# Attention-and-FFN kernel: a new order of some steps around the first two feed-forward groups, one low part moved from GpSimd to VectorE, and the last output stored in halves

## The chip, the cores and the metric

The kernel runs on one core of one Trainium2 chip. The metric is the device time of one launch in microseconds (us). The kernel before took 103.91 us, the median of three runs.

## The reference

The input x has 16 sequences of 128 tokens with 256 channels. The layer adds a weighted running mean over time (an RWKV "wkv" recurrence whose keys are the normalised x and whose values are `ctx_2048`), and then a gated feed-forward block with 704 hidden channels:

```python
# per sequence; k = layernorm(x), v = ctx_2048, C = 256 channels
def step(carry, kv_t):                      # over the 128 tokens
    aa, bb, pp = carry
    ww = u + kt
    q = maximum(pp, ww)
    y_t = (exp(pp - q) * aa + exp(ww - q) * vt) / (exp(pp - q) * bb + exp(ww - q))
    ...
x = x + wkv(time_decay, time_first, layernorm(x), ctx_2048)
n = layernorm(x)
g = (n @ gate_w.T) * gate_s                 # 704 hidden channels, weights -1, 0 or 1
u = (n @ up_w.T) * up_s
x = x + ((silu(g) * u) @ down_w.T) * down_s
```

## The kernel before

**Tiling.** Two sequences make a unit (256 tokens; 8 units), two units make a group (512 tokens; 4 groups). The 704 hidden channels are 5 full tiles of 128 and one rest of 64. A hidden tile has a running number n, from 0 to 23 over the whole program: group n // 6, tile n % 6 within it; 5, 11, 17 and 23 are the rests.

**Attention part of unit u.** ScalarE: `expk(u)` makes the exponentials `ek`. TensorE transposes them (`e_T(u)`, into `ps_a`) and, for units 0 to 3, also their products with v (`p_T(u)`, into `ps_b`; units 4 to 7 use VectorE's `mulp(u)` for that). VectorE runs two scans over time (`scan_e`, `scan_p`) and forms `denom(u)` and `numer(u)`. ScalarE makes the reciprocal (`log_den`, `recip`), GpSimd multiplies (`divide(u)`) and adds to the residual (`add_y(u)`).

**Second layernorm of unit u.** TensorE transposes the sum back (`x1_T(u)`), VectorE takes its statistics (`stats2`, `aggr2`), GpSimd and ScalarE form scale and bias, ScalarE normalises (`norm2(u)`), TensorE transposes again (`n_T(u)`). The result is kept as two float32r numbers: ScalarE copies it into the high part `xh` (`high_n(u)`), VectorE subtracts that from the original and writes the low part `xl` (`low_n(u)`).

**Feed-forward part.** For tile n TensorE multiplies high and low parts by the gate and the up weights (`gate(n)`, `up(n)`, four matmuls each, into a ring of three PSUM banks `ps_f`), ScalarE takes the silu, VectorE multiplies (`gated(n)`, into `h`), ScalarE makes the high part of the result (`high_h(n)`, into `hh`), GpSimd the low part (`low_h(n)`, into `hl`); for the rest tiles VectorE makes the low part (`low_rest(n)`, into `hx`). `down(n)` adds both parts' products to `ps_d`, which has two halves of 128 output channels, c = 0 and c = 1. From n = 20 on `down(n)` does c = 0 alone and `downb(n)` does c = 1. At the end of a group VectorE adds the result to `xc` (`residual`), and SyncE's queue stores it, one DMA per half. Of the first three products (gate 0, up 0, gate 1) the first 256 tokens are done ahead of the others, as `gatea(0)`, `upa(0)`, `gatea(1)`; these need only unit 0.

**What sets the order.** Each engine runs a list written out by hand, in its own queue, and waits on semaphores. An instruction that waits holds up all that stands behind it on its engine. The waits that matter here:

- `p_T(u)` waits until `numer(u - 1)` is done, since it overwrites `ps_b`; `e_T(u)` waits for `denom(u - 1)` in the same way.
- `gatea(0)` waits for `low_n(0)`; the other half of `gate(0)` waits for `low_n(1)`; `gate(6)`, the first of the next group, waits for `low_n(3)`.
- `gated(n)` waits for `up(n)` and the silu. A product waits until the ring's bank that it takes has been read: `gate(2)` for `gated(0)`, `gate(3)` for `gated(1)`, `gate(7)` for `low_rest(5)`.
- `down(22)` waits for the low part of tile 22; `down(23)` and `downb(23)` for `low_rest(23)`.

Of the kernel before, what the change touches and what calls it, by code (L numbers as in the profile page):

```python
# [51 lines left out]
HS = 4  # L52
# [5 lines left out]
def build(nc, x_tok, x_ch, v_tok, v_ch, w_gu, w_d, vecs, out_ch):  # L58
    with ExitStack() as ctx:  # L59
# [6 lines left out]
        def sem(name):  # L66
            return ctx.enter_context(nc.semaphore(name))
# [147 lines left out]
        def wait_low(eng, n):  # L215

            g, m = divmod(n, MC)
            if m < FULL:
                eng.wait_ge(s_hl, FULL * g + m + 1)
            else:  # L220
                eng.wait_ge(s_hx, g + 1)
# [3 lines left out]
        @block.sync  # L225
        def _(sp):
            def load_x(u):
                sp.dma_start(xt[:, seqs(u), :], x_tok[seqs(u), :, :].rearrange("b t c -> t b c")).then_inc(s_xt[u], 16)  # L228

            def load_v(k):  # L230

                g = k - GU + 1
                if k < GU or g < TOK_UNITS // GU:
                    bs = seqs(k) if k < GU else slice(g * GU * UB, (g + 1) * GU * UB)
                    sp.dma_start(vt[:, bs, :], v_tok[bs, :, :].rearrange("b t c -> t b c")).then_inc(s_vt[k], 16)
                else:
# [24 lines left out]
        def _(pool):
# [104 lines left out]
            rstd2(3); bias1(7); low_h(4); divide(4); add_y(4); rstd2(4); divide(5); add_y(5); low_h(6); low_h(7)  # L366
            rstd2(5); low_h(8); first(3); divide(6); add_y(6); low_h(9); low_h(10); rstd2(6); divide(7); add_y(7)
            low_h(12); low_h(13); rstd2(7); low_h(14); low_h(15); low_h(16); low_h(18); low_h(19); low_h(20)
            low_h(21); low_h(22)

        @block.scalar
        def _(act):
# [115 lines left out]

            rstd1(0); expk(0); elift_(); rstd1(1); expk(1); rstd1(3); log_den(0); expk(2); recip(0); wcheck(0)
            log_den(1); recip(1); wcheck(1); wcheck(2); log_den(2); recip(2); expk(3); rstd2a(0); rstd1(5); rstd2a(1)  # L490
            norm2(0); norm2(1); expk(4); high_n(0); log_den(3); high_n(1); expk(5); recip(3); tables(SILU); silu(0)
            silu(1); high_h(0); norm2(2); silu(2); high_h(1); silu(3); high_h(2); high_n(2); silu(4); high_h(3)
            silu(5); tables(LN_EXP); log_den(4); rstd1(7); high_h(4); recip(4); norm2(3); expk(6); high_n(3); expk(7)
            log_den(5); high_h(5); recip(5); tables(SILU); silu(6); silu(7); norm2(4); high_h(6); silu(8); high_n(4)
            high_h(7); silu(9); tables(LN_EXP); log_den(6); recip(6); high_h(8); norm2(5); tables(SILU); silu(10)
            high_n(5); high_h(9); silu(11); high_h(10); silu(12); high_h(11); tables(LN_EXP); log_den(7); recip(7)
            tables(SILU); silu(13); norm2(6); silu(14); high_n(6); high_h(12); silu(15); high_h(13); high_h(14)
# [5 lines left out]
        def _(dve):  # L503
# [115 lines left out]
            def gated(n):  # L619
# [6 lines left out]
                if m < FULL and n >= HS and (n - HS) % MC < FULL:  # L626
# [4 lines left out]
                nc.vector.scalar_tensor_tensor(h[:, n % HS, :] if m < FULL else up, up, vec[r, V_US + m:V_US + m + 1],  # L631
                                               sil[r, n % 2, :], ALU.mult, ALU.mult).then_inc(s_h, 1)

            def low_rest(n):
                wait_high(dve, n)
                if n >= MC:
                    dve.wait_ge(s_dn, CC * (n - MC + 1))
                nc.vector.tensor_tensor(hx[0:REST, :], ps_f[REST:P, slot(n, 1) % RING, :], hx[REST:P, :].bitcast(F32),
                                        ALU.subtract).then_inc(s_hx, 1)

            def residual(g, c):
                ts = slice(g * GT, (g + 1) * GT)
                nc.vector.scalar_tensor_tensor(xc[:, c, ts], ps_d[:, c, :], vec[:, V_DS + c:V_DS + c + 1],
                                               xc[:, c, ts], ALU.mult, ALU.add).then_inc(s_fin, 1)

            def finish(g):
# [5 lines left out]
            def finish_c(c):  # L652

                dve.wait_ge(s_x1, UNITS)
                dve.wait_ge(s_tail[c], 1)
                residual(GROUPS - 1, c)

            lift_(); stats1(0); aggr1(0); stats1(1); stats1(2); decay_(); aggr1(1); aggr1(2); stats1(3); scan_e(0)
            aggr1(3); denom(0); scan_p(0); scan_e(1); numer(0); denom(1); scan_p(1); scan_e(2); numer(1); denom(2)
            stats1(4); stats1(5); stats2(0); aggr1(4); aggr1(5); aggr2(0); stats2(1); publish(); aggr2(1); scan_e(3)  # L660
            scan_p(2); denom(3); numer(2); stats1(6); low_n(0); scan_p(3); low_n(1); numer(3); stats2(2); mulp(4)
            aggr2(2); gated(0); gated(1); scan_p(4); scan_e(4); gated(2); stats1(7); gated(3); low_n(2); numer(4)
            denom(4); aggr1(6); stats2(3); aggr1(7); aggr2(3); gated(4); gated(5); mulp(5); scan_e(5); scan_p(5)
            denom(5); low_n(3); numer(5); stats2(4); low_rest(5); aggr2(4); scan_e(6); gated(6); mulp(6); gated(7)
            finish(0); low_n(4); denom(6); stats2(5); aggr2(5); gated(8); gated(9); scan_p(6); numer(6); scan_e(7)
            low_n(5); gated(10); gated(11); mulp(7); stats2(6); denom(7); low_rest(11); gated(12); aggr2(6); scan_p(7)
            numer(7); gated(13); finish(1); low_n(6); gated(14); stats2(7); aggr2(7); gated(15); gated(16); gated(17)
            low_n(7); low_rest(17); gated(18); gated(19); finish(2); gated(20); gated(21); gated(22); gated(23)
            low_rest(23); finish_c(0); finish_c(1)

        @block.tensor
        def _(pe):
# [92 lines left out]
            def rest_of_program(exact):  # L765
                def gate(n):
                    product(n, 0, exact, 1 if slot(n, 0) < HALVED else None)

                def up(n):
                    product(n, 1, exact, 1 if slot(n, 1) < HALVED else None)  # L770

                def gatea(n):
                    product(n, 0, exact, 0)

                def upa(n):
                    product(n, 1, exact, 0)
# [72 lines left out]
```

## Time and profile before

| what | value |
|---|---|
| median of three runs | 103.91 us (103.79 to 104.14) |
| the profiled execution | 104.59 us, of which its span is 102.7 us |
| PE (TensorE) busy | 91.5 us, 89% of the span |
| DVE (VectorE) busy | 80.0 us, 78% |
| ACT (ScalarE) busy | 78.2 us, 76% |
| POOL (GpSimd) busy | 66.8 us, 65% |

All times within the span count from its start. PE's matmuls are pipelined: the printed duration of one is longer than the distance to the next, so its pace is read from start to start. On ACT and DVE an instruction may start some 0.1 us before the end printed for the one ahead of it.

### The profile page before, as it was taken

How to read it: one execution, taken by the hardware profiler on the slowest of the kernel's cores; microseconds unless marked ns; L12 is line 12 of the kernel's file. 1: busy time of each engine (PE TensorE's matmuls, PEld its weight loads, DVE VectorE, ACT ScalarE, POOL GpSimd, SP SyncE). 2: the span in 40 equal slices, each digit the busy share in tenths (PEclk: the TensorE clock that was granted, in tenths of full speed). 3: DMA queues.
4: the chain of work that ended last, by engine and by line, in shares of the span. 5: the costliest groups of instructions: out<-in, count | busy, mean ns of one | idle time of the engine just before them, and what ended most of it. 6: DMA issues, size and time to landing. Idle time of an engine off the chain costs nothing.

```text
span 102.7 us, 1698 instructions
## 1 busy us (share of the span) xinstructions
PE 91.5 (89%) x504; PEld 75.1 (73%) x504; DVE 80.0 (78%) x169; ACT 78.2 (76%) x136; POOL 66.8 (65%) x96
## 2 busy tenths in 40 slices
PE   3958976998799999996999999999999999999930
PEld 3957965996596778875788887887888778888610
DVE  1789899969998999799999998999863806543450
ACT  4371999989997879999999999999959634655300
POOL 2016465998799999894399779827899701764500
PEclk9999999999999999999999999999999999999999
DMA  1999999999000000000005000000500000400005
GB/s 32 307 379 405 403 321 388 343 387 343 34 0 0 0 0 10 0 0 0 0 0 203 1 6 0 0 3 0 203 1 0 0 6 3 183 21 0 0 28 189
DMA packets 6475, 10.78 MB, mean 105 GB/s; under 512 B 576, under 2 KB 3648, under 8 KB 6336
## 3 DMA queue, kind: packets, MB, share of 16 engines
q1 hardware_dynamic: 6320, 10.62, 28.9%
q8 instruction: 6, 0.10, 0.4%
q10 hardware_dynamic: 144, 0.03, 0.2%
q14 instruction: 5, 0.04, 0.1%
HBM read 8.55 MB, written 2.10 MB: 104 GB/s over the span
## 4 chain that ended last, share of the span: by engine, by line
PE 27%; POOL 17%; ACT 15%; issue 14%; DMA 11%; DVE 6%; SPq 4%; POOLq 2%; DVEq 1%; ACTq 0%
PE ps_f L728 16%; DMA xc<-x_ch 11%; POOL hl L346 11%; PE ps_d L745 4%; ACT ek L405 4%; PE ps_f L756 3%; ACT L374 2%; POOL xc L311 2%; ACT nt L434 2%; SPq L228 2%; PE ps_x L698 2%; ACT xh L445 2%; DVE h L631 1%; POOL rs L323 1%; POOLq L59 1%
## 5 line engine op out<-in xcount | busy, mean ns | idle before, releaser
L728 PE MATMUL ps_f<-xh,wgu_r 128*128 128x512 f32 (+1 forms) x94 | 36.3, 391 | 0.6 <-DVE xl L616 0.4
L728 PE MATMUL ps_f<-xl,wgu_r 128*128 128x512 f32 (+1 forms) x94 | 35.1, 378 | 0.0
L346 POOL TENSOR_TENSOR hl<-h,hh 128x512 fp32r<-128x512 f32 x20 | 25.6, 1293 | 9.3 <-ACT hh L476 9.2
L631 DVE SCALAR_TENSOR_TENSOR h<-ps_f,vec,sil 128x512 f32<-128x512 f32 x20 | 14.9, 744 | 9.2 <-PE ps_f L728 6.2
L728 PEld LDWEIGHTS ps_f<-xh,wgu_r 128*128 128x128 f32 x94 | 17.7, 188 | 5.5 <-issue 1.4
L728 PEld LDWEIGHTS ps_f<-xl,wgu_r 128*128 128x128 f32 x94 | 17.7, 188 | 2.8
L756 PE MATMUL ps_f<-ident 128*128 128x128 f32 x110 | 15.5, 296 | 1.9 <-POOL ident L266 1.6
L465 ACT ACTIVATE sil<-ps_f,vec 128x512 f32<-128x512 f32 x20 | 13.7, 688 | 4.0 <-PE ps_f L728 3.8
L745 PE MATMUL ps_d<-hh,wd_r 128*128 128x512 f32 x40 | 16.3, 407 | 0.1
L756 PEld LDWEIGHTS ps_f<-ident 128*128 128x128 f32 x110 | 14.5, 211 | 2.1 <-POOL ident L266 1.6
L476 ACT ACTIVATE hh<-h 128x512 fp32r<-128x512 f32 x20 | 12.5, 629 | 4.6 <-DVE h L631 4.5
L745 PE MATMUL ps_d<-hl,wd_r 128*128 128x512 f32 x40 | 15.7, 393 | 0.0
L305 POOL TENSOR_TENSOR yk<-num,rden 128x508 f32<-128x508 f32 x8 | 10.2, 1281 | 2.1 <-DVE num L593 1.5
L374 ACT ACT_TABLE_LOAD x8 | 10.3, 1283 | 1.3 <-PEq L843 1.2
L405 ACT ACTIVATE ek<-xt,nb,rs 128x256 f32<-128x256 f32 x16 | 8.7, 595 | 2.9 <-POOL nb L283 2.8
L311 POOL TENSOR_TENSOR xc<-xc,yk 128x508 f32<-128x508 f32 x8 | 10.3, 1282 | 0.6
L558 DVE TENSOR_TENSOR_SCAN sbe<-decay,ps_a 128x512 f32<-128x512 f32 x8 | 9.6, 1204 | 0.4 <-PE ps_a L679 0.4
L569 DVE TENSOR_TENSOR_SCAN sbp<-decay,ps_b 128x512 f32<-128x512 f32 x8 | 9.6, 1205 | 0.0
L745 PEld LDWEIGHTS ps_d<-hh,wd_r 128*128 128x128 f32 x40 | 7.5, 188 | 2.2 <-POOL hl L346 0.7
L745 PEld LDWEIGHTS ps_d<-hl,wd_r 128*128 128x128 f32 x40 | 7.5, 189 | 1.4
L434 ACT ACTIVATE nt<-ps_x,nb,rs 128x256 f32<-128x256 f32 x14 | 7.1, 557 | 0.8 <-POOL nb L327 0.7
L679 PE MATMUL ps_a<-ident,ek 128*128 128x128 f32 x32 | 5.1, 281 | 2.4 <-ACT ek L405 2.2
(73 smaller groups left out, 133.8 us busy)
## 6 DMA issues: line engine op xcount, KB each, us to landing
xt<-x_tok SPq DMA_DIRECT2D x8, 256.0 KB, 7.3
xc<-x_ch SPq DMA_DIRECT2D x4, 512.0 KB, 9.6
out_ch<-xc SPq DMA_DIRECT2D x8, 256.0 KB, 2.5
wgu<-w_gu SPq DMA_DIRECT2D x1, 1408.0 KB, 8.6
vc<-v_ch SPq DMA_DIRECT2D x2, 512.0 KB, 9.4
wd<-w_d SPq DMA_DIRECT2D x1, 768.0 KB, 10.0
vt<-v_tok SPq DMA_DIRECT2D x2, 256.0 KB, 5.3
vt<-v_tok SPq DMA_DIRECT2D x1, 512.0 KB, 12.3
```

What stands on the lines that cost most here:

```text
L305: nc.gpsimd.tensor_tensor(yk[:, u % 2, :, 1:T], num[:, u % 2, :, 1:T], rden[:, u % 2, :, 1:T], ALU.mult).then_inc(s_y, 1)
L311: nc.gpsimd.tensor_tensor(later(xc, u), later(xc, u), yk[:, u % 2, :, 1:T].rearrange("p (c b) t -> p c b t", c=CC), ALU.add).then_inc(s_x1, 1)
L346: nc.gpsimd.tensor_tensor(hl[:, m, :], h[:, n % HS, :], hh[:, m, :].bitcast(F32), ALU.subtract).then_inc(s_hl, 1)
L374: nc.scalar.preload_act_table_set(name)
L405: last = nc.scalar.activation(ek[:, b, :], xt[:, b, :], ACT.Exp, scale=rs1[:, b:b + 1], bias=nb1[:, b:b + 1])
L465: nc.scalar.activation(sil[:, n % 2, :], f, ACT.Silu, scale=vec[:, V_GS + m:V_GS + m + 1]).then_inc(s_sil, 1)
L476: nc.scalar.activation(hh[:, m, :], h[:, n % HS, :], ACT.Copy).then_inc(s_hh, 1)
L558: nc.vector.tensor_tensor_scan(sbe[:, u % 2, :, :].rearrange("p q t -> p (q t)"), decay[:, :, :].rearrange("p q t -> p (q t)"), ps_a[:, :, ...
L631: nc.vector.scalar_tensor_tensor(h[:, n % HS, :] if m < FULL else up, up, vec[r, V_US + m:V_US + m + 1], sil[r, n % 2, :], ALU.mult, ALU.m ...
L728: last = nc.tensor.matmul(ps_f[:, i % RING, ts], w, a, start=c == 0 and x is xh, stop=c == CC - 1 and x is xl)
L745: last = nc.tensor.matmul(ps_d[:, c, :], wd_r[:, m, cs] if exact else wd[:, m, cs], a if exact else a.bitcast(F32), start=m == 0 and i == ...
L756: nc.tensor.matmul(ps_f[:, RING - 1, 0:P], ident[:, :], ident[:, :], start=True, stop=True)
```

## The change

Five things are edited.

1. **First group, ScalarE and VectorE.** `high_n(0)` now stands ahead of `expk(4)`, and `high_n(1)` ahead of `log_den(3)`. On VectorE `low_n(0)` stands ahead of `numer(2)`, and `low_n(1)` ahead of `scan_p(3)`; `stats1(6)` moves behind `scan_p(3)`.
2. **First group, TensorE.** `e_T(4)` moves from ahead of `p_T(3)` to behind `upa(0)`, and `x1_T(2)` from ahead of `gate(0)` to behind `gate(1)`.
3. **Second group.** `low_n(3)` stands ahead of `denom(5)`, `high_h(5)` ahead of `log_den(5)`, and `gate(6)` ahead of `e_T(6)` and `x1_T(4)`.
4. **Last low part.** The low part of tile 22 is made by VectorE, in a new function `low_last`, with its own semaphore `s_hld`.
5. **End.** The products for c = 0 of tile 23 are done ahead of those for c = 1 of tile 22. The last residual for c = 1 is added and stored in two halves of 256 tokens.

```diff
+LOW_DVE = 22
...
+            if n == LOW_DVE:
+                eng.wait_ge(s_hld, 1)
+            elif m < FULL:
                 eng.wait_ge(s_hl, FULL * g + m + 1)
...
+            for i, (c, a, b) in enumerate(((0, 0, GT), (1, 0, UT), (1, UT, GT))):
+                sp.wait_ge(s_fin, done + i + 1)
+                store(c, slice(last + a, last + b))
...
-            low_h(21); low_h(22)
+            low_h(21)
...
-            norm2(0); norm2(1); expk(4); high_n(0); log_den(3); high_n(1); expk(5); recip(3); tables(SILU); silu(0)
+            norm2(0); norm2(1); high_n(0); expk(4); high_n(1); log_den(3); expk(5); recip(3); tables(SILU); silu(0)
...
-            log_den(5); high_h(5); recip(5); tables(SILU); silu(6); silu(7); norm2(4); high_h(6); silu(8); high_n(4)
+            high_h(5); log_den(5); recip(5); tables(SILU); silu(6); silu(7); norm2(4); high_h(6); silu(8); high_n(4)
...
+            def low_last(n):
+
+                g, m = divmod(n, MC)
+                wait_high(dve, n)
+                dve.wait_ge(s_dn, CC * (n - MC + 1))
+                nc.vector.tensor_tensor(hl[:, m, :], h[:, n % HS, :], hh[:, m, :].bitcast(F32),
+                                        ALU.subtract).then_inc(s_hld, 1)
...
+                if c == 0:
+                    residual(GROUPS - 1, c)
+                else:
+                    residual(GROUPS - 1, c, slice(0, UT))
+
+            def finish_d(c):
+
+                residual(GROUPS - 1, c, slice(UT, GT))
...
-                warm(2); n_T(0); warm(1); n_T(1); e_T(4); p_T(3); gatea(0); upa(0); gatea(1); x1_T(2); gate(0); gate(1); up(0); up(1)
+                warm(2); n_T(0); warm(1); n_T(1); p_T(3); gatea(0); upa(0); e_T(4); gatea(1); gate(0); gate(1); x1_T(2); up(0); up(1)
...
-                downb(22); down(23); downb(23)
+                down(23); downb(22); downb(23)
```

VectorE around the low parts of the first group, before (`den` is `denom(3)`, the two `num` are `numer(2)` and `numer(3)`, `st<-xt` is `stats1(6)`, the two `xl` are `low_n(0)` and `low_n(1)`, `sbp` is `scan_p(3)`, `st<-ps_x` is `stats2(2)`):

```order
L583 SCALAR_TENSOR_TENSOR den<-ps_a,fcol,sbe 128x2x127 x2
L593 SCALAR_TENSOR_TENSOR num<-ps_b,fcol,sbp 128x2x127 x2
L533 BN_STATS st<-xt 128x6 x2
L616 TENSOR_TENSOR xl<-ps_x,xh 128x2x256
L569 SCALAR_TENSOR_TENSOR sbp<-decay,ps_b 128x512
L616 TENSOR_TENSOR xl<-ps_d,xh 128x2x256
L593 SCALAR_TENSOR_TENSOR num<-ps_b,fcol,sbp 128x2x127 x2
L600 BN_STATS st<-ps_x 128x6 x2
```

The same place in the changed kernel (its line numbers are higher):

```order
L594 SCALAR_TENSOR_TENSOR den<-ps_a,fcol,sbe 128x2x127 x2
L627 TENSOR_TENSOR xl<-ps_x,xh 128x2x256
L604 SCALAR_TENSOR_TENSOR num<-ps_b,fcol,sbp 128x2x127 x2
L627 TENSOR_TENSOR xl<-ps_d,xh 128x2x256
L580 SCALAR_TENSOR_TENSOR sbp<-decay,ps_b 128x512
L544 BN_STATS st<-xt 128x6 x2
L604 SCALAR_TENSOR_TENSOR num<-ps_b,fcol,sbp 128x2x127 x2
L611 BN_STATS st<-ps_x 128x6 x2
```

`low_n(0)` has moved ahead of `numer(2)`, `low_n(1)` ahead of the scan, and `stats1(6)` behind it; the number of instructions is the same.

TensorE at the start of the second group, before (`ps_d<-` is `down(4)`, then `e_T(6)`, `x1_T(4)`, and the first two matmuls of `gate(6)`):

```order
L745 MATMUL ps_d<-hh,wd_r 128x512
L745 MATMUL ps_d<-hl,wd_r 128x512
L679 MATMUL ps_a<-ident,ek 128x128 x4
L698 MATMUL ps_x<-ident,xc 128x128 x4
L728 MATMUL ps_f<-xh,wgu_r 128x512
L728 MATMUL ps_f<-xl,wgu_r 128x512
```

The same place in the changed kernel:

```order
L771 MATMUL ps_d<-hh,wd_r 128x512
L771 MATMUL ps_d<-hl,wd_r 128x512
L754 MATMUL ps_f<-xh,wgu_r 128x512
L754 MATMUL ps_f<-xl,wgu_r 128x512
L754 MATMUL ps_f<-xh,wgu_r 128x512
L754 MATMUL ps_f<-xl,wgu_r 128x512
L705 MATMUL ps_a<-ident,ek 128x128 x4
L724 MATMUL ps_x<-ident,xc 128x128 x4
```

The four matmuls of `gate(6)` now stand ahead of both sets of transposes.

## Rows read from the trace of the kernel before

**Rows 1.** Windows: length, busy time (and instructions) of each engine, clock, DMA share, GB/s.

```profile
48.26:96.60 48.34, 48.34 (x229) 39.06 (x227) 35.49 (x63) 38.28 (x59) 31.91 (x38) 1.00 0.09 34
```

**Rows 2.** Timeline of ACT, first group: start, duration, engine, line, instruction.

```profile
25.31 1.09 ACT L405 ACTIVATE ek<-xt,nb,rs 128x256 f32<-128x256 f32 x2
26.30 0.59 ACT L445 ACTIVATE xh<-ps_x 128x512 fp32r<-128x512 f32 x1
...
30.88 1.27 ACT L465 ACTIVATE sil<-ps_f,vec 128x512 f32<-128x512 f32 x2
```

**Rows 3.** Timeline of DVE, first group.

```profile
25.80 0.86 DVE L593 SCALAR_TENSOR_TENSOR num<-ps_b,fcol,sbp 128x254 f32<-128x254 f32 x2
...
27.24 0.67 DVE L616 TENSOR_TENSOR xl<-ps_x,xh 128x512 fp32r<-128x512 f32 x1
27.83 1.21 DVE L569 TENSOR_TENSOR_SCAN sbp<-decay,ps_b 128x512 f32<-128x512 f32 x1
...
30.32 0.75 DVE L600 BATCH_NORM_STATS2 st<-ps_x 128x6 f32<-128x256 f32 x2
...
31.86 0.72 DVE L631 SCALAR_TENSOR_TENSOR h<-ps_f,vec,sil 128x512 f32<-128x512 f32 x1
```

**Rows 4.** Timeline of PE, first group; brackets give idle time before.

```profile
26.95 0.60 PE L688 MATMUL ps_b<-ident,vt 128*128 128x128 f32 x4
27.97 0.39 PE L728 MATMUL ps_f<-xh,wgu_r 128*128 128x256 f32 x1 [0.42 <-DVE xl L616]
...
29.49 0.61 PE L698 MATMUL ps_x<-ident,xc 128*128 128x128 f32 x4
29.86 0.36 PE L728 MATMUL ps_f<-xh,wgu_r 128*128 128x256 f32 x1
...
32.73 0.47 PE L728 MATMUL ps_f<-xh,wgu_r 128*128 128x512 f32 x1
...
33.90 0.47 PE L728 MATMUL ps_f<-xh,wgu_r 128*128 128x512 f32 x1
```

**Rows 5.** Timeline of PE, second group.

```profile
47.28 0.63 PE L679 MATMUL ps_a<-ident,ek 128*128 128x128 f32 x4 [0.85 <-ACT ek L405]
...
48.26 0.48 PE L728 MATMUL ps_f<-xh,wgu_r 128*128 128x512 f32 x1
...
50.18 0.40 PE L728 MATMUL ps_f<-xh,wgu_r 128*128 128x512 f32 x1
```

**Rows 6.** Timeline of ACT, second group.

```profile
45.67 0.58 ACT L445 ACTIVATE xh<-ps_x 128x512 fp32r<-128x512 f32 x1
```

**Rows 7.** Timeline of DVE, second group.

```profile
46.28 0.85 DVE L583 SCALAR_TENSOR_TENSOR den<-ps_a,fcol,sbe 128x254 f32<-128x254 f32 x2
47.05 0.68 DVE L616 TENSOR_TENSOR xl<-ps_x,xh 128x512 fp32r<-128x512 f32 x1
...
49.33 0.69 DVE L638 TENSOR_TENSOR hx<-ps_f,hx 64x512 fp32r<-64x512 f32 x1
```

**Rows 8.** Timeline of POOL, PEld and PE at the end.

```profile
95.48 1.30 POOL L346 TENSOR_TENSOR hl<-h,hh 128x512 fp32r<-128x512 f32 x1 [1.89 <-ACT hh L476]
...
96.39 0.39 PE L745 MATMUL ps_d<-hl,wd_r 128*128 128x512 f32 x1
96.83 0.19 PEld L745 LDWEIGHTS ps_d<-hh,wd_r 128*128 128x128 f32 x1 [0.49 <-POOL hl L346]
...
97.86 0.63 PE L745 MATMUL ps_d<-hx,wd_r 128*128 128x512 f32 x2
```

**Rows 9.** Timeline of DVE at the end.

```profile
96.21 0.69 DVE L638 TENSOR_TENSOR hx<-ps_f,hx 64x512 fp32r<-64x512 f32 x1 [0.66 <-ACT hx L478]
98.36 1.41 DVE L643 SCALAR_TENSOR_TENSOR xc<-ps_d,vec,xc 128x512 f32<-128x512 f32 x2 [1.46 <-PE ps_d L745]
```

**Rows 10.** The page, DMA issues: instruction, count, size of each, median us to landing.

```profile
out_ch<-xc SPq DMA_DIRECT2D x8, 256.0 KB, 2.5
```

**Rows 11.** Windows just before the end: columns as in the first group.

```profile
100.00:100.50 0.50, 0.00 (x0) 0.00 (x0) 0.00 (x0) 0.00 (x0) 0.00 (x0) 1.00 1.00 373
```

More of the change, by code:

```diff
@@ L156, in build @@
             "s_gate", "s_up", "s_sil", "s_h", "s_hh", "s_hhp", "s_hl", "s_hx", "s_dn", "s_fin", "s_set", "s_res"))
+        s_hld = sem("s_hld")
         s_tail = [sem(f"s_tail{c}") for c in range(CC)]
@@ L217, in wait_low @@
             g, m = divmod(n, MC)
-            if m < FULL:
+            if n == LOW_DVE:
+                eng.wait_ge(s_hld, 1)
+            elif m < FULL:
                 eng.wait_ge(s_hl, FULL * g + m + 1)
@@ L248, in _, with store @@
             load_x(6); load_x(7); load_v(4); load_res(2); load_res(3)
-            for g in range(GROUPS):
+            def store(c, ts):
+                sp.dma_start(out_ch[c * P:(c + 1) * P, ts], xc[:, c, ts]).then_inc(s_out, 16)
+            for g in range(GROUPS - 1):
                 for c in range(CC):
@@ L255, in _ @@
                         sp.wait_ge(s_fin, CC * (g - len([i for i in FIN_ACT if i < g])) + c + 1)
-                    sp.dma_start(out_ch[c * P:(c + 1) * P, g * GT:(g + 1) * GT],
-                                 xc[:, c, g * GT:(g + 1) * GT]).then_inc(s_out, 16)
-            sp.wait_ge(s_out, 16 * GROUPS * CC)
+                    store(c, slice(g * GT, (g + 1) * GT))
+            done = CC * (GROUPS - 1 - len(FIN_ACT))
+            last = (GROUPS - 1) * GT
+            for i, (c, a, b) in enumerate(((0, 0, GT), (1, 0, UT), (1, UT, GT))):
+                sp.wait_ge(s_fin, done + i + 1)
+                store(c, slice(last + a, last + b))
+            sp.wait_ge(s_out, 16 * (GROUPS * CC + 1))
         @block.gpsimd
@@ L639, in low_rest, with residual @@
                                         ALU.subtract).then_inc(s_hx, 1)
-            def residual(g, c):
-                ts = slice(g * GT, (g + 1) * GT)
-                nc.vector.scalar_tensor_tensor(xc[:, c, ts], ps_d[:, c, :], vec[:, V_DS + c:V_DS + c + 1],
+            def residual(g, c, cols=slice(0, GT)):
+                ts = slice(g * GT + cols.start, g * GT + cols.stop)
+                nc.vector.scalar_tensor_tensor(xc[:, c, ts], ps_d[:, c, cols], vec[:, V_DS + c:V_DS + c + 1],
                                                xc[:, c, ts], ALU.mult, ALU.add).then_inc(s_fin, 1)
@@ L655, in finish_c @@
                 dve.wait_ge(s_tail[c], 1)
-                residual(GROUPS - 1, c)
+                if c == 0:
[4 more added lines that the diff above has]
+                residual(GROUPS - 1, c, slice(UT, GT))
             lift_(); stats1(0); aggr1(0); stats1(1); stats1(2); decay_(); aggr1(1); aggr1(2); stats1(3); scan_e(0)
@@ L660, in _ @@
             stats1(4); stats1(5); stats2(0); aggr1(4); aggr1(5); aggr2(0); stats2(1); publish(); aggr2(1); scan_e(3)
-            scan_p(2); denom(3); numer(2); stats1(6); low_n(0); scan_p(3); low_n(1); numer(3); stats2(2); mulp(4)
+            scan_p(2); denom(3); low_n(0); numer(2); low_n(1); scan_p(3); stats1(6); numer(3); stats2(2); mulp(4)
             aggr2(2); gated(0); gated(1); scan_p(4); scan_e(4); gated(2); stats1(7); gated(3); low_n(2); numer(4)
             denom(4); aggr1(6); stats2(3); aggr1(7); aggr2(3); gated(4); gated(5); mulp(5); scan_e(5); scan_p(5)
-            denom(5); low_n(3); numer(5); stats2(4); low_rest(5); aggr2(4); scan_e(6); gated(6); mulp(6); gated(7)
+            low_n(3); denom(5); numer(5); stats2(4); low_rest(5); aggr2(4); scan_e(6); gated(6); mulp(6); gated(7)
             finish(0); low_n(4); denom(6); stats2(5); aggr2(5); gated(8); gated(9); scan_p(6); numer(6); scan_e(7)
@@ L668, in _ @@
             low_n(7); low_rest(17); gated(18); gated(19); finish(2); gated(20); gated(21); gated(22); gated(23)
-            low_rest(23); finish_c(0); finish_c(1)
+            low_last(22); low_rest(23); finish_c(0); finish_c(1); finish_d(1)
         @block.tensor
@@ L782, in downb @@
                     down_(n, exact, (1,))
-                warm(2); n_T(0); warm(1); n_T(1); e_T(4); p_T(3); gatea(0); upa(0); gatea(1); x1_T(2); gate(0); gate(1); up(0); up(1)
+                warm(2); n_T(0); warm(1); n_T(1); p_T(3); gatea(0); upa(0); e_T(4); gatea(1); gate(0); gate(1); x1_T(2); up(0); up(1)
                 gate(2); gate(3); up(2); up(3); n_T(2); gate(4); gate(5); x1_T(3); down(0); up(4); e_T(5); down(1)
-                down(2); down(3); n_T(3); down(4); e_T(6); x1_T(4); gate(6); up(6); gate(7); down(5); up(7); gate(8)
+                down(2); down(3); n_T(3); down(4); gate(6); e_T(6); x1_T(4); up(6); gate(7); down(5); up(7); gate(8)
                 n_T(4); gate(9); up(8); x1_T(5); down(6); up(9); e_T(7); gate(10); gate(11); down(7); n_T(5); up(10)
```

## The prediction

> **What bounds the kernel now.** I read the windows first. From 48.26 us to 96.60 us TensorE is busy for 48.34 us of 48.34 at full clock, while VectorE is busy for 35.49 and ScalarE for 38.28 [rows 1]. So from 48.26 on the end is set by two things: when TensorE enters this run, and what follows it. Time lost ahead of 48.26 is not won back inside the run, since there is no idle time in it. Then I read the timelines of the three places that the edits touch. Ahead of the run the engines wait for each other in turn, and a step that is late on one is late on all; the chain of waits runs there through ScalarE, TensorE and VectorE.
>
> **First group: what the new order does.** On ScalarE `expk(4)` starts at 25.31 and `high_n(0)` at 26.30 [rows 2]. Swapped, `high_n(0)` starts at 25.31 and ends 0.59 later, at 25.90. That is 0.99 us earlier. What ScalarE has to do before the first silu is the same work in another order, so that silu stays near 30.88 [rows 2].
>
> On VectorE `numer(2)` starts at 25.80 in the kernel before [rows 3]. Now `low_n(0)` is ahead of it and waits for the high part, to 25.97 (a hand-over of 0.07, my estimate from rows that sit between 0.04 and 0.11). It holds the engine for 27.83 - 27.24 = 0.59 [rows 3], so `numer(2)` runs from 26.56 to 27.42, which is 0.76 later than before.
>
> On TensorE the queue still has `p_T(3)` ahead of `gatea(0)`, and `p_T(3)` waits for `numer(2)`. It starts at 27.48 instead of 26.95 [rows 4]. Four transposes hold TensorE for some 0.49, so `gatea(0)` starts at 27.97. It started at 27.97 before [rows 4]. The early low part buys nothing here: another wait takes the place of the one removed.
>
> Behind it the queue has now three half products and `e_T(4)`, then two half products, then `x1_T(2)`. Three half products took 29.49 - 27.97 = 1.52 with a slow first one, and then about 0.47 each; a set of transposes takes 29.86 - 29.49 = 0.37 [rows 4], and the first product behind one about 0.55. The sum: 27.97 + 0.55 + 0.47 + 0.37 + 0.55 + 0.47 + 0.47 = 30.85, the start of `x1_T(2)`. It was 29.49 [rows 4]. Its input is no tighter: `add_y(2)` is late by the 0.76 of `numer(2)`, which would allow 30.25. The last transpose ends 0.61 after the first began, at 31.46 [rows 4].
>
> VectorE takes the statistics behind it. They started at 30.32, and `gated(0)` at 31.86 [rows 3], so 1.54 lie between, with `mulp(4)` among it. Now: 31.46 + 0.04 + 1.54 = 33.04 for `gated(0)`, 1.18 later. `gate(2)` needs the bank that `gated(0)` reads; it started 0.15 behind the end of that, 32.73 [rows 3, 4], and now starts at 33.04 + 0.72 + 0.15 = 33.91. `gate(3)` had to wait until 33.90 for `gated(1)` [rows 4]; now `gated(1)` is done by about 34.5 and `gate(3)` follows `gate(2)` at once, at 33.91 + 1.0 = 34.91. As it starts without a pause it saves 0.1 of the start-up. So TensorE is **0.91 us late** from here. From here to 48.26 the steps hang on each other (silu on the gate product, gated on both, the next product on gated), so I let it pass on in full. Bounds: 0.58, if `x1_T(2)` cost nothing and only `numer(3)`, done at about 30.85, held the statistics back; 1.18 if the pause before `gate(3)` stays.
>
> **Second group.** ScalarE's high part of unit 3 ends at 45.67 + 0.58 = 46.25 [rows 6], and VectorE reaches this place at 46.28 [rows 7]. In the new order `low_n(3)` goes first, from 46.32 to 47.00, and `gate(6)` starts at 47.06 instead of 48.26 [rows 5]. That fills 0.85 of idle time [rows 5]. But `e_T(6)` and `x1_T(4)` stand behind it: `gate(6)` holds TensorE for 1.0, the first transposes 0.35, so `x1_T(4)` starts at 48.41 and ends 0.61 later, at 49.02. VectorE's `stats2(4)` starts at 49.05 and takes 0.75 [rows 3], then `low_rest(5)` runs from 49.84 to 50.53; it ran from 49.33 to 50.02 [rows 7]. `gate(7)` must wait for it. `up(6)` is done by 49.8, but `gate(7)` starts only at 50.6 instead of 50.18 [rows 5]; with the start-up after a pause TensorE is **0.50 us late**, on top of the other. The early `high_h(5)` does not help, since the statistics stand ahead of `low_rest(5)` and not it. Bounds: 0 (the place is hidden if `low_rest(5)` needs nothing of `x1_T(4)`; it does by the queue) and 0.6.
>
> **End.** GpSimd's low part of tile 22 runs from 95.48 to 96.78; TensorE is free at 96.39 + 0.23 = 96.62 and waits to 96.83 for it [rows 8]. VectorE sits idle for 0.66 before 96.21 [rows 9], that is from 95.55. A low part there takes 0.67 to 0.69 [rows 3, 7] with one input in PSUM; this one has both in SBUF, and no row shows that on VectorE. I take 0.69: from 95.5 to 96.2, holding the engine for 0.60, so `low_rest(23)` keeps its 96.21 and `down(22)` starts at 96.62. Bounds: 0.67, and GpSimd's 1.30 [rows 8], which would make `low_rest(23)` 0.6 late. The Trainium skill speaks against this edit: GPSIMD Engine Reference, Key points, says that GpSimd and VectorE contend for SBUF when a VectorE instruction has two SBUF inputs. By that rule the 1.30 would be nearer if GpSimd were at work; its list ends with tile 21 now, so nothing of its own is running.
>
> Then c = 0: two matmuls of tile 22 and one of 23, 96.62 + 3 x 0.23 = 97.31 free, result at 97.48; its residual starts at 97.58, half of 1.41 long [rows 9], to 98.28. For c = 1 three more matmuls end at 98.17. The first half of its residual starts at 98.28. Two pieces of 254 took 0.86 [rows 3], so both halves are done at 98.28 + 0.86 = 99.14. Before, the last residual ended at 98.36 + 1.41 = 99.77 [rows 9]. That is 0.63 won, of which 0.21 comes from the low part, and the rest from c = 0 no longer being in the way of c = 1.
>
> The last store has half the size. A store of 256 KB lands 2.5 us after issue [rows 10]; at 373 GB/s [rows 11] 128 KB are 0.35 us of it. I take 0.35; at least nothing is won. The skill's DMA: Bandwidth & Descriptors (Anatomy of one DMA) gives a fixed part of some 2.0 us and bytes over 436e9: by it the half is worth 0.30, a sum 0.05 higher than mine. Together **0.98 us won**.
>
> **The sum.** 0.91 + 0.50 - 0.98 = +0.43 us. The profiled execution took 104.59 for a span of 102.7; it would take 105.0. That execution is 0.7% above the median of 103.91, so the median goes to 103.91 + 0.43 = 104.34. One part in 300, 0.31 us, is about what a measurement of this kernel can tell from no change; +0.43 is just beyond it.
>
> **The rivals.**
> - *The wait in the first group is hidden* (faster). Place: between 33 and 46 us. If ScalarE's chain to the second group (exponentials, high part, 25 to 46 us) and not TensorE's products were what really sets 48.26, the 0.91 is absorbed where ScalarE still has work in hand. For it: ScalarE is on the chain of waits for most of this stretch. Against it: ScalarE's own silus there wait for the products. It decides at a slack of 0.91 between the first gated tiles and ScalarE's next exponentials. Sum 0.50 - 0.98 = -0.48: 103.4; with both slips absorbed -0.98: 102.9.
> - *The second group costs nothing*, since statistics of unit 4 come early enough or `gate(7)` is not held. Sum 0.91 - 0.98 = -0.07: 103.8. For it: 0.85 of TensorE's idle time is filled. It decides at `low_rest(5)` ending by the time that `up(6)` is done.
> - *The end gives less*: the half store lands no sooner, +0.78: 104.7. With a slow low part on VectorE (1.30) the 0.21 is lost and c = 0 waits 0.5 for `low_rest(23)`: about 105.1.
> - *The moves do nothing*: the waits only change places and no start moves. That is the first rival with both slips absorbed, 102.9, and its chance is in there.
>
> **Chances.** Both slips and the gain at the end: 0.50, with its own range 104.0 to 104.8. Absorbed, one or both: 0.21. No cost in the second group: 0.17. The end gives less: 0.12. Within the likeliest case some 0.12 falls under 104.22, the border of slower. So slower 0.38 + 0.12 = 0.50; within 0.3% 0.12 + 0.15 = 0.27, as most of the third case is there; faster 0.21 + 0.02 = 0.23. The range goes down into the first rival and up to the last: 103.1 to 104.9.
>
> **What the profile will show.** Right: `gatea(0)` starts where it did, near 28.0; `x1_T(2)` near 30.9; `gated(0)` near 33.0; TensorE idle about 1 us before `gate(2)`; `gate(6)` well ahead of `e_T(6)`, then idle time of some 0.8 before `gate(7)` with `low_rest(5)` as its releaser; no idle time before `down(22)`; the last residual half 0.6 sooner behind the last matmuls. Wrong: TensorE's unbroken run starts no more than 0.5 later than 48.26 and 50.18 did, or `gated(0)` starts before 32.3. What would upset it most is that TensorE, held up early, had slack that I do not see, or that a set of transposes ends sooner than modelled.

## The result

The changed kernel is slower: 105.09 us (median of five runs) against 104.03 us, a ratio of 1.0104 with a 95% interval of 1.0079 to 1.0128, or 0.82 to 1.33 us. The ratio compares means, and leaves out one execution of each kernel (105.54 and 106.77 us) that took some 1.5 us longer than the others. Forecast were 104.34 us, 0.43 us more than before, and a range of 103.1 to 104.9. So the direction was right, but the size was too small by more than half, and the time lies above the range. The profiled execution took 105.4 us with a span of 103.6 us.

The first group in the changed kernel, timeline of VectorE (start, duration, engine, line, instruction; brackets: idle time before and its releaser). These rows answer to [rows 3].

```profile
26.04 0.68 DVE L627 TENSOR_TENSOR xl<-ps_x,xh 128x512 fp32r<-128x512 f32 x1
26.64 0.86 DVE L604 SCALAR_TENSOR_TENSOR num<-ps_b,fcol,sbp 128x254 f32<-128x254 f32 x2
...
31.55 0.76 DVE L611 BATCH_NORM_STATS2 st<-ps_x 128x6 f32<-128x256 f32 x2 [0.54 <-PE ps_x L724]
...
33.11 1.38 DVE L642 SCALAR_TENSOR_TENSOR h<-ps_f,vec,sil 128x512 f32<-128x512 f32 x2
```

The same in TensorE's timeline; they answer to [rows 4].

```profile
27.64 0.63 PE L714 MATMUL ps_b<-ident,vt 128*128 128x128 f32 x4 [1.48 <-DVE num L604]
28.03 0.37 PE L754 MATMUL ps_f<-xh,wgu_r 128*128 128x256 f32 x1
...
30.92 0.60 PE L724 MATMUL ps_x<-ident,xc 128*128 128x128 f32 x4
...
33.97 0.47 PE L754 MATMUL ps_f<-xh,wgu_r 128*128 128x512 f32 x1 [1.06 <-DVE h L642]
...
34.97 0.39 PE L754 MATMUL ps_f<-xh,wgu_r 128*128 128x512 f32 x1
```

The reader sees the steps of the forecast one by one. `low_n(0)` ends early, but `p_T(3)` waits 1.48 us for `numer(2)`, so `gatea(0)` starts at 28.03 and not earlier than in [rows 4]. `x1_T(2)` starts at 30.92 (forecast 30.85), VectorE waits 0.54 for it, `gated(0)` starts at 33.11 (forecast 33.04), and TensorE is idle for 1.06 us before `gate(2)`.

The second group, TensorE and VectorE, for [rows 5] and [rows 7]:

```profile
48.00 0.50 PE L754 MATMUL ps_f<-xh,wgu_r 128*128 128x512 f32 x1 [0.60 <-DVE xl L627]
...
51.66 0.50 PE L754 MATMUL ps_f<-xh,wgu_r 128*128 128x512 f32 x1 [0.64 <-DVE hx L657]
```

```profile
50.11 0.76 DVE L611 BATCH_NORM_STATS2 st<-ps_x 128x6 f32<-128x256 f32 x2 [0.61 <-PE ps_x L724]
50.91 0.69 DVE L657 TENSOR_TENSOR hx<-ps_f,hx 64x512 fp32r<-64x512 f32 x1
```

`gate(6)` starts at 48.00, earlier than in [rows 5] although all around it is late. But then VectorE waits 0.61 us for `x1_T(4)` before its statistics, `low_rest(5)` is late behind them, and TensorE waits 0.64 us for it before `gate(7)`. What was filled is given back, and more.

The end, VectorE and TensorE, for [rows 8] and [rows 9]:

```profile
97.15 0.69 DVE L650 TENSOR_TENSOR hl<-h,hh 128x512 fp32r<-128x512 f32 x1
97.88 0.69 DVE L657 TENSOR_TENSOR hx<-ps_f,hx 64x512 fp32r<-64x512 f32 x1
99.24 1.57 DVE L662 SCALAR_TENSOR_TENSOR xc<-ps_d,vec,xc 128x512 f32<-128x512 f32 x3 [0.67 <-PE ps_d L771]
```

```profile
98.18 0.39 PE L771 MATMUL ps_d<-hh,wd_r 128*128 128x512 f32 x1
98.41 0.40 PE L771 MATMUL ps_d<-hl,wd_r 128*128 128x512 f32 x1
98.64 0.49 PE L771 MATMUL ps_d<-hx,wd_r 128*128 128x512 f32 x1
```

TensorE goes on without a pause into `down(22)`. And the stores (instructions with least, median and longest duration in ns, then issue to landing), followed by the page's DMA issues for the halves; they answer to [rows 10]:

```profile
L255 SPq DMA_DIRECT2D out_ch<-xc x9: 332/332/611, 55.8 to 101.1; - x9
...
DMA to landing us min/median/max: 2.1/2.5/2.5
```

```profile
out_ch<-xc SPq DMA_DIRECT2D x2, 128.0 KB, 2.3
```

The last residual ends at 99.24 + 1.57 = 100.81, but the last store is issued only at 101.1. The issue of the first half took 611 ns instead of 332. Looked at one by one, this half landed 2.5 us after its issue, and the second, whose issue took 446 ns, landed 2.1 us after its own; the 2.3 above is the middle of the two.

**Marks.** Executions differ by up to 1 us in when the first `norm2` starts, with the same program ahead of it. So I compare distances between marks within each trace: A is the start of `norm2(0)` on ScalarE, B the first matmul of `down(0)`, C the first of `down(5)`, D the start of the last group's residuals, E their end, F the end of the span. In the kernel before, A, B and C are

```profile
23.50 1.02 ACT L434 ACTIVATE nt<-ps_x,nb,rs 128x256 f32<-128x256 f32 x2
```

```profile
39.66 0.48 PE L745 MATMUL ps_d<-hh,wd_r 128*128 128x512 f32 x1
...
51.12 0.62 PE L745 MATMUL ps_d<-hx,wd_r 128*128 128x512 f32 x2
```

and in the changed one

```profile
23.52 1.02 ACT L445 ACTIVATE nt<-ps_x,nb,rs 128x256 f32<-128x256 f32 x2
```

```profile
40.64 0.48 PE L771 MATMUL ps_d<-hh,wd_r 128*128 128x512 f32 x1
...
52.69 0.62 PE L771 MATMUL ps_d<-hx,wd_r 128*128 128x512 f32 x2
```

All distances, in us, each the difference of two starts or ends in that kernel's trace:

| kernel | A to B | B to C | C to D | D to E | E to F | ratio (interval) |
|---|---|---|---|---|---|---|
| before | 16.16 | 11.46 | 47.24 | 1.41 | 2.93 | 1 |
| changed | 17.12 | 12.05 | 46.55 | 1.57 | 2.79 | 1.0104 (1.0079 to 1.0128) |
| e1 first group | 17.14 | 11.46 | 47.25 | 1.41 | 4.87 | 1.0073 (1.0044 to 1.0102) |
| e2 second group | 16.16 | 12.09 | 47.23 | 1.41 | 2.89 | 1.0028 (1.0000 to 1.0056) |
| e3 both groups | 17.14 | 12.04 | 47.22 | 1.41 | 2.92 | 1.0148 (1.0112 to 1.0185) |
| e4 end | 16.16 | 11.51 | 46.53 | 1.58 | 2.96 | 0.9947 (0.9917 to 0.9977) |
| e5 end, no halves | 16.15 | 11.51 | 46.54 | 1.45 | 2.84 | 0.9958 (0.9928 to 0.9988) |
| e6 halves alone | 16.14 | 11.46 | 47.22 | 1.53 | 4.49 | 1.0079 (1.0019 to 1.0140) |
| e7 half on ScalarE's queue | 16.16 | 11.48 | 46.51 | 1.57 | 2.83 | 0.9940 (0.9921 to 0.9958) |
| e8 second, rest first | 16.15 | 11.16 | 47.51 | 1.41 | 4.53 | 0.9990 (0.9960 to 1.0021) |
| e9 first, numer(2) first | 16.69 | 11.47 | 47.23 | 1.41 | 2.94 | 1.0059 (1.0007 to 1.0111) |
| e10 first, x1_T(2) early | 16.74 | 11.53 | 47.25 | 1.41 | 2.97 | 1.0061 (1.0038 to 1.0085) |
| e11 both back | 16.16 | 11.46 | 47.23 | 1.41 | 2.96 | 1.0101 (1.0011 to 1.0192) |
| e12 end, gated(0) first | 16.40 | 11.44 | 46.55 | 1.45 | 2.99 | 0.9958 (0.9940 to 0.9976) |

The distances from A to E repeat within 0.05 us where the program is the same; E to F does not. The span is printed to a tenth, so E to F is good to 0.05 us only. In e1, e6 and e8 the profiled execution is one in which the last store landed 4.0 to 4.5 us after its issue instead of 2.1 to 2.7, and E to F there says nothing of the edit.

### The profile page after: what moved, and what is told of

Same layout as the page of the kernel before. It is cut to its first block, busy times and chain, and to the rows that moved or that the text cites. A ratio compares the mean times of both kernels' runs of the same rounds, so it can differ in the third digit from the quotient of the medians.

```text
span 103.6 us, 1700 instructions
## 1 busy us (share of the span) xinstructions
PE 90.8 (88%) x504; PEld 75.0 (72%) x504; DVE 81.0 (78%) x171; ACT 78.0 (75%) x136; POOL 65.6 (63%) x95
## 4 chain that ended last, share of the span: by engine, by line
PE 65%; DMA 11%; DVE 11%; issue 4%; SPq 4%; POOL 1%; DVEq 0%; POOLq 0%
PE ps_f L754 39%; PE ps_d L771 16%; DMA xc<-x_ch 11%; PE ps_x L724 3%; PE ps_f L782 3%; PE ps_x L732 2%; SPq L232 2%; PE ps_a L705 2%; DVE st L611 1%; DVE sbp L580 1%; DVE xl L627 1%; POOL xc L322 1%; DVE xc L662 1%; SPq L239 1%; DVE sbe L569 1%
## 5 line engine op out<-in xcount | busy, mean ns | idle before, releaser
L357 POOL TENSOR_TENSOR hl<-h,hh 128x512 fp32r<-128x512 f32 x19 | 24.3, 1293 | 7.4 <-ACT hh L487 7.3
L604 DVE SCALAR_TENSOR_TENSOR num<-ps_b,fcol,sbp 128x254 f32<-128x254 f32 x16 | 6.9, 470 | 0.2
```

## The experiments

My theory: the slips of the first and of the second group add up, since TensorE has no idle time behind them, and the end gives some of it back. Rivals: one of the slips is absorbed, or the early `gate(6)` is a gain, or the end gives nothing.

**e1, the first group alone.** ScalarE's, VectorE's and TensorE's lists of edits 1 and 2:

```diff
-            scan_p(2); denom(3); numer(2); stats1(6); low_n(0); scan_p(3); low_n(1); numer(3)
+            scan_p(2); denom(3); low_n(0); numer(2); low_n(1); scan_p(3); stats1(6); numer(3)
...
-  n_T(1); e_T(4); p_T(3); gatea(0); upa(0); gatea(1); x1_T(2); gate(0); gate(1); up(0)
+  n_T(1); p_T(3); gatea(0); upa(0); e_T(4); gatea(1); gate(0); gate(1); x1_T(2); up(0)
```

> The kernel before with edits 1 and 2 alone (the first group's order on ScalarE, VectorE and TensorE). My theory: numer(2) behind low_n(0) and x1_T(2) behind gate(1) hold up gated(0) by 1.2 us, and of it 0.98 reaches TensorE's unbroken run, so this is slower by 0.98 us, a ratio near 1.0095. Rival A (the first wait is absorbed ahead of 48 us and the loss lies in the second group): within 0.2 us of before.

Measured: 1.0073 (1.0044 to 1.0102), A to B longer by 17.14 - 16.16 = 0.98 us, and the rest of the way to E as before. The slip is passed on in full. The rival in which it is absorbed has fallen.

**e2, the second group alone.**

```diff
-            denom(5); low_n(3); numer(5); stats2(4); low_rest(5)
+            low_n(3); denom(5); numer(5); stats2(4); low_rest(5)
...
-            log_den(5); high_h(5); recip(5)
+            high_h(5); log_den(5); recip(5)
...
-                down(4); e_T(6); x1_T(4); gate(6); up(6)
+                down(4); gate(6); e_T(6); x1_T(4); up(6)
```

> The kernel before with edit 3 alone (low_n(3) ahead of denom(5), high_h(5) ahead of log_den(5), gate(6) ahead of e_T(6) and x1_T(4)). My theory: gate(7) waits for low_rest(5) and starts 0.5 us later than before, so slower by 0.5 us, ratio near 1.005. Rival A: this edit carries nearly all of the loss, slower by 1.4 us or more. Rival B (the filled idle time of 0.85 us is a gain): faster by 0.4 us.

Measured: 1.0028 (1.0000 to 1.0056), B to C longer by 0.63 us. Both rivals are out: it carries neither nearly all nor is it a gain. TensorE's timeline shows the trade, 0.49 idle before `gate(6)` and 0.64 before `gate(7)`:

```profile
46.28 0.50 PE L728 MATMUL ps_f<-xh,wgu_r 128*128 128x512 f32 x1 [0.49 <-DVE xl L616]
...
49.94 0.50 PE L728 MATMUL ps_f<-xh,wgu_r 128*128 128x512 f32 x1 [0.64 <-DVE hx L638]
```

**e3, both groups.** The edits of e1 and e2 together.

> Edits 1, 2 and 3 without those at the end. If the two slips add up, as TensorE's run has no idle time: 0.98 + 0.5 = 1.48 us slower, ratio near 1.0142. Rival (they overlap, since both are waits of the same engines): 1.0 us slower, ratio 1.0096.

Measured: 1.0148 (1.0112 to 1.0185). By the marks 0.98 + 0.58 = 1.56 us, a ratio of 1.015. They add up; an overlap (1.0096) lies outside the interval.

**e4, the end alone.** Edits 4 and 5.

> Edits 4 and 5 alone (low part of tile 22 on VectorE, c = 0 of tile 23 first, last residual and store in halves). Predicted blind: 0.98 us faster. From the profile of the changed kernel I now expect less, 0.55 to 0.65 us faster (ratio near 0.994), since the store of the first half held SyncE's queue for 0.61 us instead of 0.33 and the three residuals took 1.57 us. Rival (the end gives nothing, and the loss of the whole is smaller in front): within 0.2 us of before.

Measured: 0.9947 (0.9917 to 0.9977). By the marks C to D is shorter by 0.71, D to E longer by 0.17 and E to F longer by 0.03: 0.51 us won, not the 0.98 of the forecast. The ratio makes 0.55 us, the lower edge of what was expected here. Its stores show one issue of 791 ns.

```profile
L255 SPq DMA_DIRECT2D out_ch<-xc x9: 332/333/791, 53.8 to 99.3; - x9
```

**e5, the end without halves.**

```diff
-            low_h(21); low_h(22)
+            low_h(21)
...
-            low_rest(23); finish_c(0); finish_c(1)
+            low_last(22); low_rest(23); finish_c(0); finish_c(1)
...
-                downb(22); down(23); downb(23)
+                down(23); downb(22); downb(23)
```

> Edit 4 and the order of c = 0 and c = 1, but the last residual and store whole. If the gain of the end is the wait for GpSimd and the earlier residual of c = 0, and the halves give little because SyncE's queue is held 0.6 to 0.8 us by a store: 0.5 us faster than before, the same as all of the end's edits. If the halves carry their computed 0.35 us: only 0.2 us faster.

Measured: 0.9958 (0.9928 to 0.9988). By the marks 0.70 won from C to D and 0.04 lost in the residuals. From A to the end of the span it is shorter than before by (102.7 - 23.50) - (101.4 - 22.91) = 0.71 us, where e4 with halves has (102.7 - 23.50) - (101.8 - 23.06) = 0.46. The times of e4 and e5 can't be told apart, so the gain of the end is the low part on VectorE and the new order, and the halves are worth nothing that shows. No run separates the low part from the order. By the rows the low part is worth the idle 0.21 of [rows 8], and the order two products of 0.23 that no longer stand ahead of c = 0: 0.67 of the 0.70.

**e6, the halves alone.** The residual and store for c = 1 in halves on the kernel before.

> Only the last residual and store for c = 1 in halves, products in the old order and GpSimd's low part. My first figure for it: 0.35 us faster, less one more start-up on VectorE of 0.08. Theory now: the issue of the first half takes 0.6 to 0.8 us instead of 0.33 and holds the second back, so within 0.15 us of before.

Measured: 1.0079 (1.0019 to 1.0140). The interval excludes the gain of 0.35, but it says little. By the marks D to E is 0.12 longer, and the longest issue took 454 ns. The rest of the profiled execution's loss comes from a last store that landed late. Its six times run from 103.96 to 105.78, four of them above 105; but of the kernel before, 5 of 11 executions measured beside it are above 105 too. So the late landings need not be the work of the halves. Its lowest time, 103.96, is no gain over the kernel before (lowest 103.69).

**e7, one half issued from ScalarE's queue.**

```diff
+            act.wait_ge(s_fin, CC * (GROUPS - 1) + 2)
+            act.dma_start(out_ch[P:2 * P, (GROUPS - 1) * GT:(GROUPS - 1) * GT + UT],
+                          xc[:, 1, (GROUPS - 1) * GT:(GROUPS - 1) * GT + UT]).then_inc(s_out, 16)
```

> All of the end's edits, but the first half of the last store is issued from ScalarE's queue, so that it does not stand ahead of the second half in SyncE's. If the long issue in SyncE's queue is what ate the gain: another 0.2 to 0.4 us faster than with all on SyncE's queue, that is 0.8 us faster than before, with the last issue within 0.1 us of the last residual. If the issues hold each other up wherever they are issued from: no better than 0.53 us faster.

Measured: 0.9940 (0.9921 to 0.9958), 103.33 us, the lowest median of all. The last store on SyncE's queue is issued at 98.8, right behind the last residual (97.20 + 1.57 = 98.77), and no issue is long. So in e4 it was the long issue that held back the issue of the second half. But the forecast of another 0.2 to 0.4 us did not come true: E to F is shorter by 0.13 than in e4 and not shorter than in the changed kernel (2.83 against 2.79), and the intervals of e4, e5 and e7 overlap. With nothing in its way the half lands 2.4 us after its issue, where the whole store of before lands 2.5 us after its own. The 0.35 of the forecast are missing here too, so it is not the long issue that ate them.

```profile
L255 SPq DMA_DIRECT2D out_ch<-xc x8: 332/332/360, 53.8 to 98.8; - x8
...
DMA to landing us min/median/max: 2.3/2.4/2.5
```

The traffic shows where they went. Here is, for the kernel before, e5, e7, the changed kernel and e4, the stretch of 1.5 us that begins 0.83 us behind the first issue of the last group, that for c = 0 (columns as in [rows 1]; the last two are the share of the DMA engines and GB/s):

```profile
99.97:101.47 1.50, 0.00 (x0) 0.00 (x0) 0.00 (x0) 0.00 (x0) 0.00 (x0) 1.00 0.96 348
```

```profile
98.71:100.21 1.50, 0.00 (x0) 0.00 (x0) 0.00 (x0) 0.00 (x0) 0.00 (x0) 0.81 0.94 348
```

```profile
98.80:100.30 1.50, 0.00 (x0) 0.00 (x0) 0.00 (x0) 0.00 (x0) 0.00 (x0) 1.00 1.00 343
```

```profile
100.84:102.34 1.50, 0.00 (x0) 0.00 (x0) 0.00 (x0) 0.00 (x0) 0.00 (x0) 1.00 0.92 323
```

```profile
98.87:100.37 1.50, 0.00 (x0) 0.00 (x0) 0.00 (x0) 0.00 (x0) 0.00 (x0) 1.00 0.80 283
```

In the first three the bytes of all the last group's stores, 2 x 256 KB, leave in one stream that keeps the DMA engines full: 343 to 348 GB/s for 1.5 us are 515 to 522 of their 524 thousand bytes. The last store, whole or half, is issued when the engines are already full or about to be with the bytes for c = 0, and waits for its turn. What then sets the end is the first issue: from it to the end of the span it takes 3.56 us before (102.7 - 99.14), 3.52 in e5, 3.63 in e7 and 3.59 in the changed kernel. It takes 3.76 in e4, whose stream is thinner (283 GB/s) behind the issue of 791 ns. I read this from the traces; no run issues the half with free engines, so what its smaller size would be worth there is not measured.

**e8, the second group with low_rest(5) ahead of the statistics.**

```diff
-            low_n(3); denom(5); numer(5); stats2(4); low_rest(5); aggr2(4)
+            low_n(3); denom(5); numer(5); low_rest(5); stats2(4); aggr2(4)
```

> Edit 3 alone, with low_rest(5) ahead of stats2(4) on VectorE. If gate(7) is late in the second group only because low_rest(5) stands behind statistics that wait for transposes moved behind gate(6): the wait of 0.64 us before gate(7) is gone and the kernel is 0.1 to 0.3 us faster than before, ratio 0.997 to 0.999. If something else holds gate(7) (the silu, the ring): slower by 0.3 us as with edit 3 as it is.

Measured: 0.9990 (0.9960 to 1.0021). The wait before `gate(7)` is gone and B to C is 0.30 shorter than before, 0.93 shorter than in e2. So the place of `low_rest(5)` behind the statistics is what made the second slip. The expected gain of 0.1 to 0.3 us did not come, though: C to D is 0.27 longer, and B to D is the same as before within 0.03. The cause: TensorE now reaches `up(7)` ahead of the silu of tile 6 and waits there for ScalarE, as the weight loads show.

```profile
49.82 0.41 PEld L745 LDWEIGHTS ps_d<-hx,wd_r 128*128 128x128 f32 x2
50.67 0.19 PEld L728 LDWEIGHTS ps_f<-xh,wgu_r 128*128 128x128 f32 x1 [0.43 <-ACT sil L465]
```

**e9, e10 and e11, the first group's two causes.** In e9 `numer(2)` goes back ahead of `low_n(0)`, in e10 `x1_T(2)` goes back behind `gatea(1)`, in e11 both.

```diff
 e9, e11
-            scan_p(2); denom(3); low_n(0); numer(2); low_n(1); scan_p(3); stats1(6)
+            scan_p(2); denom(3); numer(2); low_n(0); low_n(1); scan_p(3); stats1(6)
 e10, e11
-            gatea(1); gate(0); gate(1); x1_T(2); up(0)
+            gatea(1); x1_T(2); gate(0); gate(1); up(0)
```

> Edits 1 and 2 alone, but numer(2) stands again ahead of low_n(0) on VectorE (low_n(1) behind it, then the scan). If numer(2) behind low_n(0) is part of the slip: p_T(3) and gatea(0) come 0.6 to 0.7 us earlier, x1_T(2) is then held by its place and by add_y(2), and from norm2(0) to down(0) the slip over the kernel before falls from 0.97 to about 0.2 us. If only the place of x1_T(2) matters: it stays at 0.9.

> Edits 1 and 2 alone, but x1_T(2) stands right behind gatea(1), as before. If its place is part of the slip: it starts when add_y(2) is done, 0.6 us earlier than in the changed kernel, and the slip from norm2(0) to down(0) falls from 0.97 to about 0.3 us. If only the late numer(2) matters: it stays at 0.9.

> Both of these: numer(2) ahead of low_n(0), and x1_T(2) behind gatea(1); high_n(0) ahead of expk(4) and low_n(0) ahead of scan_p(3) stay. If the two together make the slip, it is gone to within 0.1 us of the kernel before. If the early high part itself costs: 0.5 or more stays.

Measured, A to B over the kernel before: 0.53 in e9, 0.58 in e10, 0.00 in e11. Each of the two makes a good half of the slip, and with both undone all of it is gone, while the high part still stands ahead of `expk(4)`. So the early high part costs nothing, and gains nothing either: in e11 `gatea(0)` starts 0.65 us earlier behind A than before (26.70 - 22.88 against 27.97 - 23.50), but `x1_T(2)`, on which `gated(0)` hangs, starts where it did (28.84 - 22.88 = 5.96 us behind A, 29.49 - 23.50 = 5.99 before). In e9 VectorE waits for `x1_T(2)`, which its place in the queue holds back; in e10 `x1_T(2)` waits for `add_y(2)`, which follows the late `numer(2)`, as the bracket says.

```profile
29.40 0.66 PE L698 MATMUL ps_x<-ident,xc 128*128 128x128 f32 x4 [0.15 <-POOL xc L311]
```

The sizes 0.2 and 0.3 that I expected for e9 and e10 were too low. The two together cost 0.98 and not the sum 1.11, so they overlap in part. The ratio of e11, 1.0101 with an interval of 1.0011 to 1.0192 from four runs, does not agree with its marks: two of its four times are above 105.4 and two at 103.96 and 103.99. The two low ones are what the marks say. The time alone leaves e11 undecided.

**e12, the end without halves, and gated(0) ahead of mulp(4).**

```diff
-            numer(3); stats2(2); mulp(4); aggr2(2); gated(0); gated(1)
+            numer(3); stats2(2); aggr2(2); gated(0); mulp(4); gated(1)
```

> The kernel before with the low part of tile 22 on VectorE, c = 0 of tile 23 first and whole stores, and with gated(0) ahead of mulp(4). VectorE sets gated(0) in the kernel before, so it should start up to 0.2 us sooner: with the 0.65 us of the end some 0.8 us faster than before. If gated(0) is set by up(0) or the silu: only the 0.5 of the end, and mulp(4) late may cost 0.1.

Measured: 0.9958 (0.9940 to 0.9976), no better than e5. `gated(0)` does start earlier (8.35 us behind A, against 8.60 in e5), but `gated(1)` is late behind `mulp(4)` and `gate(3)` waits 0.21 for it; A to B is 0.24 longer. A miss: the bound only moved one tile on.

```profile
33.10 0.47 PE L740 MATMUL ps_f<-xh,wgu_r 128*128 128x512 f32 x1 [0.21 <-DVE h L635]
```

## Why the prediction was right in direction and wrong in size

**What bounds the kernel**: right. C to D is the same within 0.05 us in all kernels whose end is the same, except e8, which has a wait of its own. What is lost ahead of it is lost for good: e3 shows the sum of both slips in the time.

**The first group**: right in each step, 0.91 forecast, 0.96 measured (0.98 in e1). `gatea(0)` did not come earlier, `x1_T(2)` and `gated(0)` were late by what was worked out. e9 to e11 show that the two named causes, and nothing else, make it.

**The second group**: right in mechanism, 0.50 forecast, 0.59 measured. e8 shows the cause by removing it. My sentence that `gate(6)` "fills 0.85 of idle time" is true as well, but it was not worth anything, since the next wait was set by another chain.

**The end**: here the sum failed, and the step that failed is "128 KB are 0.35 us of it. I take 0.35". Forecast were 0.98 us won; the marks give (47.24 - 46.55) - (1.57 - 1.41) + (2.93 - 2.79) = 0.67 us. Term by term:

- The residuals starting 0.78 earlier: 0.69. The low part with both inputs in SBUF took the 0.69 that I had taken, but `low_rest(23)` could start only 0.73 behind its start and not 0.60, and the first product of `hx` then holds TensorE for 0.33 instead of 0.23.
- The residuals themselves, 0.15 longer for a third instruction: 0.16.
- The last store, "0.35 won": 0.14, and in e4 nothing. This is the step that failed most. I had priced the last store as if it moved alone. The windows under e7 show the DMA engines full with the bytes for c = 0 and c = 1 together, and the end of the span follows the first of these issues by 3.52 to 3.63 us, whether the last store is whole or in halves. [rows 11] had this sign already: a share of 1.00 at 373 GB/s. So of the 0.35 nothing was won; the 0.14 only gives back the 0.16 of the third residual, for which the end did not wait. What was won is the earlier start of the residuals, 0.69, and no more. The long issues of SyncE's queue (611 ns in the changed kernel, 791 ns in e4) come on top: nothing that shows in the changed kernel, 0.1 to 0.2 us in e4. The Trainium skill, DMA: Bandwidth & Descriptors (Anatomy of one DMA), would give an estimate of 0.30 for the smaller size; its figures are a fit for single transfers issued by GpSimd. Here, in e7, the half landed 0.1 us sooner than the whole store, and the measurement decides.

With the measured terms the sum is 0.96 + 0.59 - 0.67 = 0.88 us of span. The profiled executions differ by 105.4 - 104.59 = 0.81, and the medians by 1.06. All lie within the interval of the ratio or at its edge. Of the 0.63 us between the forecast of 0.43 and the medians' 1.06, 0.05 are the first group's, 0.09 the second's and 0.31 the end's. The 0.18 between 0.88 and 1.06 I do not assign: the spread of A (22.5 to 23.5 us between executions) is larger than that. That the profiled execution of before was a late one (104.59 against a median of 103.91) does not enter: it is late ahead of A, and the changed kernel's A is the same within 0.02. One slip in the forecast's arithmetic carries nothing: 0.31 us is 0.3% of 103.91, while one part in 300 would be 0.35.

**The rivals**: "the wait is hidden" and "the second group costs nothing" fell (e1, e2). "The end gives less" came true in its store part ("the half store lands no sooner": 0.98 - 0.35 = 0.63 against 0.67 measured), though not by the slow low part. I had given it 0.12 and treated it as a case apart, where it should have been in the sum: an end of 0.67 with the slips as forecast would have made 0.74 us, most of what was measured.

## What to carry to other kernels

An instruction moved ahead in one engine's list only helps if all that stands between it and its consumer, on every queue, comes earlier too; follow the next engine's list up to the first wait, and ask whose instruction was pushed back. Before a last store is made smaller, look whether the DMA engines are still full with the store ahead of it: if they are, the end hangs on when the first of these stores is issued, and not on the size of the last. Compare kernels by distances between marks in the traces where executions differ by more than the effect. Of the versions tried, the kernel before with the low part on VectorE and c = 0 first is the best, 0.4% to 0.6% under before (e5, and e4 and e7 with halves, which the times do not tell apart), where the change as it was made is 1.0% over it.

## What the runs showed of the hardware that was not expected

- The stores of the last group leave as one stream that fills the DMA engines: 348 GB/s over 1.5 us in the kernel before and in e5, 343 in e7 with the last store in halves. The end of the span came 3.52 to 3.63 us behind the first issue in these three and in the changed kernel.
- A store's issue in SyncE's queue took 332 to 361 ns in most cases, but more for the last ones of four kernels: 418 and 454 ns for the two halves in e6, 611 and 446 in the changed kernel, 791 and 430 in e4. e12 has no halves, and its last store's issue took 573 ns, where the same one in e5 took 332. What makes an issue long stays open.
- Stores landed 2.1 to 2.7 us after their issue, but the last one in three executions 4.0, 4.1 and 4.5 us after it (e6, e8, e1). Here are e1's stores:

```profile
L256 SPq DMA_DIRECT2D out_ch<-xc x8: 332/332/360, 54.9 to 100.6; - x8
...
DMA to landing us min/median/max: 2.3/2.4/4.5
```

- A VectorE subtraction with two inputs in SBUF took 0.69 us, against 0.67 to 0.69 with one in PSUM, with GpSimd idle beside it (its last instruction in the changed kernel ends at 95.15, the subtraction starts at 97.15). The contention of which the Trainium skill warns (GPSIMD Engine Reference, Key points) was not met, and no run here tested it.
